# The attention stage of a decoder layer: query stacks through DRAM, one inversion a batch, a ring of four PSUM banks

## What is computed

```
b, s, _ = x.shape                                   # 16, 256, 512, layer-normed
q = (x @ wq).reshape(b, s, 32, 16).transpose(0, 2, 1, 3)
k = (x @ wk).reshape(b, s, 8, 16).transpose(0, 2, 1, 3)
v = (x @ wv).reshape(b, s, 8, 16).transpose(0, 2, 1, 3)
q, k = _apply_rope(q, cos, sin), _apply_rope(k, cos, sin)
k, v = jnp.repeat(k, 4, axis=1), jnp.repeat(v, 4, axis=1)
scores = jnp.einsum('bhqd,bhkd->bhqk', q, k) / HEAD_DIM ** 0.5
scores = jnp.where(causal[None, None], scores, -jnp.inf)
out = jnp.einsum('bhqk,bhkd->bhqd', jax.nn.softmax(scores, axis=-1), v)
```

## Time and profile before

| | |
|---|---|
| runs | 3281.49 us median of 3 (3280.7 to 3293.23) |
| the profiled execution | 3280.95 us, its span 3278.8 us |
| instructions | 46466 |
| TensorE, its weight loads | 2826.2 us (86%), 2342.6 us (71%) |
| VectorE | 1325.4 us (40%) |
| ScalarE | 860.3 us (26%) |
| GpSimd | 779.9 us (24%) |
| granted clock of TensorE, mean | 0.922 |
| the stage of attention | 180 to 777 us |

### The profile page before, as it was taken

The page is one execution under the profiler, slowest core; times in us unless marked ns, Lnnn a source line. Parts: engine busy times, 40 slices in busy tenths (PEclk is TensorE's granted clock), DMA queues, the critical chain, the costliest instruction groups (busy, mean ns, idle before and its releaser), DMA issues.

```text
span 3278.8 us, 46466 instructions
## 1 busy us (share of the span) xinstructions
PE 2826.2 (86%) x16154; PEld 2342.6 (71%) x16154; DVE 1325.4 (40%) x2276; ACT 860.3 (26%) x1573; POOL 779.9 (24%) x1110
## 2 busy tenths in 40 slices
PE   7968777773978777049999999999999999999998
PEld 6843333331756665039999999999999999999997
DVE  6745555551778888411321322322313313223211
ACT  2115444451144444111221211211212212112110
POOL 4523434441332232440110111011111101110110
PEclk9968888885988898569999999999999999999999
DMA  3125555542211221320320321212212203212110
GB/s 100 35 59 92 101 95 98 94 81 57 83 65 44 71 77 43 96 75 11 99 83 26 103 69 58 87 52 77 86 31 94 93 10 110 78 49 90 45 42 22
DMA packets 116217, 228.09 MB, mean 70 GB/s; under 512 B 33038, under 2 KB 34734, under 8 KB 115952
## 3 DMA queue, kind: packets, MB, share of 16 engines
q1 hardware_dynamic: 94272, 165.43, 19.8%
q0 software_dynamic: 21808, 60.65, 6.0%
HBM read 148.77 MB, written 38.94 MB: 57 GB/s over the span
## 4 chain that ended last, share of the span: by engine, by line
PE 55%; POOL 2%; issue 1%; DMA 0%; DVE 0%; DVEq 0%; ACT 0%; POOLq 0%
PE ex_hid L1727 28%; PE ex_acc L103 9%; PE ex_acc L102 9%; PE ex_acc L104 9%; POOL slot_table_dram L1550 2%; PE ex_xb L1697 1%; DMA ex_ys<-xn_dram,ex_rows_in 0%; POOL out_dram L1579 0%; DVE ex_ys L1640 0%; POOL ex_xg L1545 0%; POOL ex_ys L1560 0%; PE ex_acc L1697 0%; DVE ex_xT0l L1623 0%; DVEq L72 0%; ACT ex_xT0h L1590 0%
## 5 line engine op out<-in xcount | busy, mean ns | idle before, releaser
L1648 DVE SCALAR_TENSOR_TENSOR ex_h0l<-ex_hid,ex_h0h 128x640 fp32r<-128x640 f32 x128 | 105.6, 825 | 690.6 <-ACT ex_h0h L1607 690.6
L1648 DVE SCALAR_TENSOR_TENSOR ex_h1l<-ex_hid,ex_h1h 128x640 fp32r<-128x640 f32 x128 | 105.5, 824 | 613.7 <-ACT ex_h1h L1607 550.2
L596 DVE TENSOR_REDUCE at_nb<-at_sc 128x2 f32<-128x512 f32 (+1 forms) x384 | 245.7, 682 | 148.3 <-PE at_sc L659 147.1
L1607 ACT ACTIVATE ex_h0h<-ex_hid 128x640 fp32r<-128x640 f32 x128 | 90.2, 704 | 739.0 <-PE ex_hid L1727 732.5
L1607 ACT ACTIVATE ex_h1h<-ex_hid 128x640 fp32r<-128x640 f32 x128 | 90.2, 704 | 737.5 <-PE ex_hid L1727 701.1
L558 ACT ACTIVATE at_pT<-at_st 128x512 f32<-128x512 f32 x384 | 208.6, 597 | 261.7 <-PE at_st L671 260.3
L102 PE MATMUL ex_acc<-ex_w_h,ex_h1h 128*128 128x512 f32 x640 | 254.1, 397 | 0.0
L102 PE MATMUL ex_acc<-ex_w_h,ex_h0h 128*128 128x512 f32 x640 | 252.9, 395 | 0.0
L103 PE MATMUL ex_acc<-ex_w_l,ex_h0h 128*128 128x512 f32 x640 | 250.6, 392 | 0.0
L103 PE MATMUL ex_acc<-ex_w_l,ex_h1h 128*128 128x512 f32 x640 | 250.6, 392 | 0.0
L104 PE MATMUL ex_acc<-ex_w_h,ex_h1l 128*128 128x512 f32 x640 | 249.9, 390 | 0.0
(11 more groups left out here) (267 smaller groups left out, 5980.7 us busy)
## 6 DMA issues: line engine op xcount, KB each, us to landing
ex_raw<-in_w_tiles_dram SPq DMA_DIRECT2D x256, 256.0 KB
at_qs<-at_qT_hi SPq DMA_DIRECT2D x256, 64.0 KB, 2.8
x_in<-in_x_dram SPq DMA_DIRECT2D x32, 256.0 KB
at_q_in<-act SPq DMA_DIRECT2D x16, 512.0 KB
at_qs<-at_qT_lo SPq DMA_DIRECT2D x128, 64.0 KB, 2.6
act<-at_raw SPq DMA_DIRECT2D x128, 64.0 KB
at_recb<-o_rec_dram SPq DMA_DIRECT2D x32, 256.0 KB
op_x<-in_x_dram SPq DMA_DIRECT2D x32, 256.0 KB
```

The lines of the kernel that those rows point to most:

```text
L596: dve.tensor_reduce(nb[e][:, r, p % 2, heads, qb], sc[n % 3][:].rearrange("p (h k) -> p h k", h=heads.stop - heads.start), AX.X, ALU.max, ...
L1607: act.activation(h[f % 2][0][:], hid[:, :, 0:HB], ACT.Relu).then_inc(sm["h_hi"], 1)
L1648: dve.scalar_tensor_tensor(h[f % 2][1][:], hid[:, :, 0:HB], 0.0, f32(h[f % 2][0][:]), ALU.max, ALU.subtract).then_inc(sm["h_lo"], 1)
```

## The change

- **Q through DRAM.** `store_q` writes the three parts of a batch (`qT_hi` twice, `qT_lo` once) to a scratch tensor `q_rows` in DRAM, one transfer of 128 rows and 512 KB each; it stands last in SyncE's step e = 0. `load_stack` waits for these stores (`q_stored`) and reads the stack of a half in two transfers of 48 rows and 384 KB. That is 3 + 4 transfers for a batch where there were 24.
- **Order of SyncE.** Q of a batch is loaded one step earlier, in e = 1, two batches ahead. The store of the inverses stands first in e = 0, the load of the denominators early in e = 1, ahead of `load_stack`; the broadcast behind the maxima in e = 0.
- **One inversion a batch.** `den` and `rec` hold both halves (128x64). VectorE inverts at p = 4 of e = 1; the broadcast goes to all 128 partitions once; GpSimd multiplies in e = 1.
- **One ring of four banks** in place of `sc` (three) and `tb`. `TURNS` gives the order of its users in a step; `taken` waits for the reader of the fourth turn before. Q is transposed at p = 1 and 3, K at p = 4 (e = 0) or 3 (e = 1).
- **TensorE's order.** In each pair the transposed scores of half h - 2 come first, then the score heads, and the mask is added last.
- The loop runs five times instead of six, and the batches 13 and 14 are unrolled.

```diff
-        den = s.sb("at_den", [P, 32])
-        rec = s.sb("at_rec", [P, 32])
+        den = s.sb("at_den", [P, 64])
+        rec = s.sb("at_rec", [P, 64])
...
-        sc = [s.ps(f"at_sc{i}", [P, D]) for i in range(3)]
+        ring = [s.ps(f"at_ring{i}", [P, D]) for i in range(4)]
         pv = s.ps("at_pv", [P, D])
-        tb = s.ps("at_tb", [P, 512])
-        o_den, o_rec = io["o_den"], io["o_rec"]
...
+        TURNS = (("s0", "s1", "m", "s2", "s3", "q0", "s4", "s5", "s6", "s7", "q1", "s8", "s9", "k", "s10", "s11"),
+                 ("s0", "s1", "m", "s2", "s3", "s4", "s5", "s6", "s7", "k", "s8", "s9", "s10", "s11"))
+
+        def bank(q, e, name):
+
+            return ring[(2 * q + TURNS[e].index(name)) % 4]
...
-            with eng.Fori(0, 6) as i:
+            with eng.Fori(0, 5) as i:
                 for k in range(2):
                     for e in range(2):
                         step(2 * i + 3 + k, i + 1 + k, 1 - k, e)
-            for j in range(15, 19):
+            for j in range(13, 19):
                 for e in range(2):
...
-            def load_stack(b, e, i, free):
+            def store_q(b, par):
                 wait_apart(sp, sm["q_hi"], 2 * b + 2, passed_sp)
                 wait_apart(sp, sm["q_lo"], 2 * b + 2, passed_sp)
+                for c in range(3):
+                    sp.dma_start(q_rows[par, :, c], f32(qT[c // 2][:]).rearrange("p h n -> p (h n)"))\
+                        .then_inc(sm["q_stored"], 16)
+
+            def load_stack(b, par, e, i, free):
+                wait_apart(sp, sm["q_stored"], 48 * b + 48, passed_sp)
                 if free is not None:
                     wait_apart(sp, sm["shifted"], free, passed_sp)
-                for u in range(UN):
-                    g = UN * e + u
-                    for c, part in enumerate((qT[0], qT[0], qT[1])):
-                        row = 64 * (u % 2) + HD * c
-                        sp.dma_start(f32(qs[i][row:row + HD, u // 2, :, :]),
-                                     f32(part[HD * g:HD * g + HD, :, :])).then_inc(q_loaded[i], 16)
+                for r in range(2):
+                    sp.dma_start(f32(qs[i][64 * r:64 * r + 48, :, :, :]).rearrange("p g h n -> p g (h n)"),
...
             def first():
                 load_q(0)
-                load_stack(0, 0, 0, None)
+                load_q(1)
+                store_q(0, 0)
+                load_stack(0, 0, 0, 0, None)
 
             def step(j, w, q, e):
                 h = 2 * j + e
-                if e == 0 and within(j + 1, 0, B):
-                    load_q(j + 1)
+                if e == 1 and within(j + 2, 0, B):
+                    load_q(j + 2)
+                if e == 0 and within(j - 3, 0, B):
+                    wait_apart(sp, sm["den_turned"], j - 3 + 1, passed_sp)
+                    wait_apart(sp, sm["recb_loaded"], 16 * (j - 3), passed_sp)
+                    sp.dma_start(o_rec.rearrange("j (a b) -> (j a) b", b=64), rec[:]).then_inc(sm["rec_stored"], 16)
+                if e == 1 and within(j - 2, 0, B):
+                    b = j - 2
+                    for i in range(2):
+                        wait_apart(sp, raw_moved[i], 80 * b + 80, passed_sp)
+                    sp.dma_start(den[:], o_den[q].rearrange("j (a b) -> (j a) b", b=64)).then_inc(sm["den_loaded"], 16)
                 if within(h + 1, 0, HALVES):
-                    load_stack(j + e, 1 - e, (2 * q + e + 1) % 4, PIECES * (h - 2) if within(h, 3, HALVES) else None)
-                if within(h - 4, 0, HALVES):
-                    wait_apart(sp, sm["den_turned"], h - 4 + 1, passed_sp)
-                    wait_apart(sp, sm["recb_loaded"], 16 * (h - 4), passed_sp)
-                    sp.dma_start(o_rec.rearrange("j (a b) -> (j a) b", b=32), rec[:]).then_inc(sm["rec_stored"], 16)
+                    load_stack(j + e, (q + e) % 2, 1 - e, (2 * q + e + 1) % 4,
+                               PIECES * (h - 2) if within(h, 3, HALVES) else None)
                 if within(h - 1, 0, HALVES):
                     wait_apart(sp, sm["m_kept"], h, passed_sp)
                     i = (2 * q + e - 1) % 4
                     for r in range(2):
                         sp.dma_start(f32(qs[i][64 * r + 48:64 * r + 49, :, :, :]).rearrange("p g h n -> p (g h n)"),
                                      f32(mT[i % 2][16 * r:16 * r + 16, :])).then_inc(m_loaded[i], 16)
+                if e == 0 and within(j - 3, 0, B):
+                    b = j - 3
+                    wait_apart(sp, sm["rec_stored"], 16 * b + 16, passed_sp)
+                    wait_apart(sp, sm["attn_done"], b, passed_sp)
+                    sp.dma_start(recb[:].rearrange("p u n -> p (u n)"),
+                                 o_rec.unsqueeze(1).to_broadcast([G, HD, TPB * D])).then_inc(sm["recb_loaded"], 16)
                 if within(h - 3, 0, HALVES):
                     i, b, x = 1 - e, j - 2 + e, raw[1 - e]
                     wait_apart(sp, sm["sums_kept"], 2 * (h - 3) + 2, passed_sp)
-                    sp.dma_start(o_den[i], x[HD:P:32, :, :].rearrange("p u n -> p (u n)")).then_inc(raw_moved[i], 16)
+                    sp.dma_start(o_den[(q + e) % 2, UN * i:UN * i + UN], x[HD:P:32, :, :].rearrange("p u n -> p (u n)"))\
+                        .then_inc(raw_moved[i], 16)
                     for u in range(UN):
                         row = 64 * i + HD * u
                         sp.dma_start(t["act"][row:row + HD, bass.ds(TPB * b, TPB), :],
                                      x[32 * u:32 * u + HD, :, :]).then_inc(raw_moved[i], 16)
-                if within(h - 4, 0, HALVES):
-                    b = j - 2
-                    wait_apart(sp, sm["rec_stored"], 16 * (h - 4) + 16, passed_sp)
-                    wait_apart(sp, sm["attn_done"], b, passed_sp)
-                    sp.dma_start(recb[64 * e:64 * e + 64, :, :].rearrange("p u n -> p (u n)"),
-                                 o_rec.unsqueeze(1).to_broadcast([UN, HD, TPB * D])).then_inc(sm["recb_loaded"], 16)
-                if within(h - 3, 0, HALVES):
-                    i, b = 1 - e, j - 2 + e
-                    wait_apart(sp, raw_moved[i], 80 * b + 80, passed_sp)
-                    sp.dma_start(den[:], o_den[i].rearrange("j (a b) -> (j a) b", b=32)).then_inc(sm["den_loaded"], 16)
+                if e == 0 and within(j + 1, 0, B):
+                    store_q(j + 1, (q + 1) % 2)
 
...
-                if e == 0 and within(j - 3, 0, B):
+                if e == 1 and within(j - 3, 0, B):
                     b = j - 3
                     for r in range(2):
                         pool.wait_ge(raw_moved[r], ONE + 80 * b + 80)
-                    pool.wait_ge(sm["recb_loaded"], ONE + 32 * b + 32)
+                    pool.wait_ge(sm["recb_loaded"], ONE + 16 * b + 16)
                     x = t["act"][:, bass.ds(TPB * b, TPB), :]
                     pool.tensor_tensor(x, x, recb[:], ALU.mult).then_inc(sm["attn_done"], 1)
...
-                    if p == 1 and within(h - 1, 0, HALVES):
+                    if p == 0 and within(h - 1, 0, HALVES):
                         act.wait_ge(sm["m_turned"], ONE + h)
-                        act.activation(mT[(e - 1) % 2][:], tb[0:32, 0:P], ACT.Copy).then_inc(sm["m_kept"], 1)
+                        act.activation(mT[(e - 1) % 2][:], bank(q, e, "m")[0:32, 0:P], ACT.Copy).then_inc(sm["m_kept"], 1)
...
-                    if e == 0 and p >= 4 and within(j + 1, 0, B):
-                        q_hi(j + 1, p - 4, [(q_loaded[(2 * q + k) % 4], 192 * w + 192) for k in range(2)])
+                    if e == 0 and p in (1, 3) and within(j + 1, 0, B):
+                        q_hi(j + 1, p // 2, bank(q, e, f"q{p // 2}"))
...
-                    if p == 1 and within(h - 4, 0, HALVES):
-                        dve.wait_ge(sm["den_loaded"], ONE + 16 * (h - 4) + 16)
-                        wait_apart(dve, sm["rec_stored"], 16 * (h - 4), passed_dve)
+                    if e == 0 and p in (1, 3) and within(j + 1, 0, B):
+                        q_lo(j + 1, p // 2, bank(q, e, f"q{p // 2}"))
+                    if p == 4 - e and within(h + 1, 0, HALVES):
+                        keep_k(h + 1, (2 * q + e + 1) % 4, bank(q, e, "k"))
+                    if e == 1 and p == 4 and within(j - 2, 0, B):
+                        dve.wait_ge(sm["den_loaded"], ONE + 16 * (j - 2) + 16)
+                        wait_apart(dve, sm["rec_stored"], 16 * (j - 2), passed_dve)
                         dve.reciprocal(rec[:], den[:]).then_inc(sm["den_turned"], 1)
-                    if p == 3 and within(h + 1, 0, HALVES):
-                        keep_k(h + 1, (2 * q + e + 1) % 4)
-                    if e == 0 and p >= 4 and within(j + 1, 0, B):
-                        q_lo(j + 1, p - 4)
...
+            def taken(j, q, e, name):
+
+                h, at = 2 * j + e, TURNS[e].index(name)
+                last, back = (TURNS[e][at - 4], 0) if at >= 4 else (TURNS[1 - e][at - 4], 1)
+                h = h - back
```

(56 more changed lines are left out.)

70 lines of the change are left out of this document (32 added, 38 removed).

## The result

The kernel after takes 3293.15 us (median of 11 runs, 3286.9 to 3299.0), the kernel before on the same chip 3279.92 us (11 runs, 3267.27 to 3293.23): a ratio of 1.0036, 95% interval 1.0023 to 1.005. So it is 13 us slower, within the 0.5% that the text ahead called no change, where 28 us less were forecast. The range held the time; the sign was wrong.

The account below looks back on a forecast made before the run. Bound before: crowded SyncE queue and full DMA engines, a 5.6 us stall, slow matmuls behind it. 15 x 31.6 + 23 = 497 against 16 x 33.1 = 530; -33 + 9 - 4 = -28 us, 3253 us; range 3165 to 3315.

Parts of the forecast that it names:

- The old stall: Attention before the change: TensorE stalled 5.6 us, passed on from VectorE's wait for the denominators' load behind a crowded SyncE queue.
- the new chain: Attention loop: Q split, stores to DRAM, stack loads, TensorE's next e=0 step; 31.6 us a batch against 33.1.
- T to the stores' issue: From TensorE's start of step e=0 (T) to SyncE's issue of the stores, behind the moves: 12.5 us.
- stores' issue to loads' issue: SyncE's queue: 1.4 us to first packet, 10.5 for the stores, 0.5 to pass the wait.
- loads' issue to TensorE: End of the loop: 1.4 us to first packet, 4.7 for the loads, 0.6 for landing and the maxima's rows.
- 8 engines at the broadcast's rate each, 150 GB/s: Stores of 1.57 MB to DRAM: eight DMA engines, each as fast as in the broadcast, 10.5 us.
- The loads' rate: Stack loads of 786 KB: 173 GB/s, as for full engines with mixed shapes, 4.7 us; bounds 2.1 to 7.3.
- T + 7 in all: Step e=0 behind a stall: TensorE reaches pair 2 at 7 us after its start, at half clock.
- T + 10.1 without a stall: Step e=0 at full clock: the stores are issued 10.1 us after TensorE's start.
- rival 2: Attention: chain of 20.7 us fits under TensorE's 23.5, so TensorE bounds, no stall; 3123 us; chance 0.10.
- The prologue and the drain: Once each: first scores at 207.9, 9 us later; drain 4 us shorter, one broadcast fewer in front of the last.
- rival 1: Slow stores: 108 GB/s, 14.6 us, batch 35.7, 3319 us; deciding from 12.25 us, the change's zero point; chance 0.20.

Follow-up runs that it names:

- e12_moves: Kernel after, with the moves of the sums behind the maxima of e=1 issued one step later, behind the next e=0's maxima: 3298.33 us, ratio 1.0053 to before.
- e1_rows: Kernel after, with each row's three parts adjacent in the scratch, so a store's DRAM side is 128 rows at one stride: 3154.42 us, ratio 0.9612 to before.
- e3_early: Kernel after, with SyncE storing Q ahead of the moves of the sums in e=0: 3289.23 us, ratio 1.002 to before.
- e10_two: Kernel after, with one of the three stores (the middle part) left out once the first batch has stored it: 3249.4 us, ratio 0.9907 to before.
- e9_qin: Kernel after, with the next Q's load issued behind the maxima of e=1, out of the stores' time: 3281.48 us, ratio 1.0008 to before.

## Why the prediction was wrong, by its own steps

- **The mechanism was right.** The old stall is gone, the new chain closes a loop of one batch, TensorE's wait stands at the first pair of e = 0 and is put down to the maxima behind the stacks, 15 times (at the middle batch for 8.5 us, not 5 to 6), the share in the stores' time is one half, the clock falls behind each wait, and the reciprocal's wait of 3.3 us at the middle batch (4 forecast) is covered.
- **The step that failed is the sum of the new chain**, 31.6 us a batch where 34.0 were measured at the middle batch and 34.6 in the mean; all three links were sized too small:

| link | predicted | middle batch | mean of fourteen | error of the mean |
|---|---|---|---|---|
| T to the stores' issue | 12.5 | 13.0 | 13.3 | 0.8 |
| stores' issue to loads' issue | 12.4 | 13.3 | 13.4 | 1.0 |
| loads' issue to TensorE | 6.7 | 7.7 | 7.9 | 1.2 |

The errors sum to 3.0 us a batch, 3.0 x 15 = 45 us on 15 batches that close the loop. The batch of the kernel before was taken too short as well: from its first scores to the maxima's transpose of its last e = 0 step (at 699.69 us) its batches take 33.4 us and not 33.1, 4 us in all. -28 + 45 - 4 = +13, the 13 measured.

- **The stores' rate.** "8 engines at the broadcast's rate each, 150 GB/s" gave 10.5 us for what took 11.4. The error is small because two larger ones met: the steady rate is higher (175 GB/s by the slope, 202 in the prologue), and 2.2 us that do not depend on the bytes were left out: the slow start, and 0.7 us for the load of the next Q, which the prediction did not count as a user of these engines. A window of 3.5 us over one short transfer, the broadcast's, could not show a start apart from a steady rate.
- **The loads' rate.** The 173 GB/s taken for full engines of mixed shapes was right: 179. At 173 GB/s, 786 KB are 4.5 us and not the 4.7 of the sum. But that counts the loads alone, and the five moves are issued from 510.52 on, while they run. Whether those make up the 1.2 to 1.4 us that are missing beside 1.4 + 4.5 + 0.6 is not shown (e12_moves).
- **The stores' place in the queue.** T + 13.0 comes after the second split, done at T + 11.5, and after the moves: the order predicted, half a microsecond late. Of that 0.3 us is a slip: the terms behind "T + 7 in all" add up to 7.3. Those of "T + 10.1 without a stall" add up to 9.9, which only rival 2 uses.
- **The prologue and the drain.** First scores at 207.68, predicted 207.9. The stage ends at 790.6 us; from the last maxima's transpose to there it is 41.7 us, against 46.6 before: -4.9, predicted -4.
- **The rivals.** TensorE-bound (3123) needed stores over all engines: e1_rows made that true and came to 3154. Its batch is 25.0 us and not 23.5, as 1.2 us of waiting is left and the 7.8 us link with it. Slow stores (rival 1) were given the deciding point of 12.25 us, worked out with the other terms fixed; with those 2.0 us larger, and the batch before 0.3, the break-even of the stores moves down to about 10.5, and 11.4 is past it. The trace shows half rate for some 4 us (102 against 202 GB/s) and then no longer. Engines that drift out of step could do that, but no run here shows which rows meet, and the cause of the slow start stays open.
- **The range and chances.** A chain that closes a loop turns each microsecond of error into 16. Three links estimated from far rows deserved an error of 2 us together, 30 us of time, as much as the whole gain that was forecast. The 3.0 us that they missed by was half as much again. That the range held the time is owed to its width and not to the sum.

## What to carry to other kernels

Count the engines of a transfer before its bytes: here a scratch layout of 8 blocks of 16 rows cost 139 us against 128 rows at one stride, with the same bytes and the same number of instructions. When a change puts a round trip through DRAM into a loop that one engine waits for, lay out the whole loop as a sum, list every other transfer that is issued during each link, and give the sum an error times the number of turns. And a moved issue in a queue is an exchange as long as what it is moved past is needed as early (e3_early, e12_moves).

## What was not expected of the hardware

- **Issues get longer behind large transfers over half of the engines.** A store's issue takes 0.65 us in e10_two, and the third in a row takes 2.61 us in the kernel after; in e10_two the third is the next Q's load, and it takes 2.37; the next Q's load takes 1.57 against 0.57 before, the four moves behind stores 5.39 against 2.59 (e3_early). With 16 engines the third store takes 0.98 (e1_rows). SyncE is held in that time, so a queue that has few issues can still be late. Engines that are backed up would explain it; no run here tests that.
- **Eight engines start at half their later rate**: 88 to 102 GB/s in the first 3 to 4 us, 181 to 202 after that, in the prologue and in the loop (e9_qin) alike. In e1_rows the same stores run at 354 GB/s, the start included.
